# Gated linear attention: output gate multiplied from PSUM by VectorE, norm weights folded into the output projection

## The reference, cut to what matters

```python
o = o_dense + o_sparse
g = (x @ Wga @ Wgb).reshape(B, L, H, DV)
o = o * lax.rsqrt(jnp.mean(o * o, axis=-1, keepdims=True) + EPS) * norm_w
o = o * (g * jax.nn.sigmoid(g))
return o.reshape(B, L, H * DV) @ Wo
```

## Time and profile before

| | |
|---|---|
| median of 3 runs | 1803.05 us (1800.98 to 1803.4) |
| profiled execution, time | 1806.19 us |
| its span, first to last instruction | 1804.9 us |
| TensorE (PE) busy | 1556.2 us, 86% |
| VectorE (DVE) busy | 1275.3 us, 71% |
| ScalarE (ACT) busy | 1098.3 us, 61% |
| GpSimd (POOL) busy | 697.8 us, 39% |
| the GLA stage in the span | about 278 to 941 us |

### The profile page before, as it was taken

The page is one execution under the profiler, slowest core; times in us unless marked ns, Lnnn a source line. Parts: engine busy times, 40 slices in busy tenths (PEclk is TensorE's granted clock), DMA queues, the critical chain, the costliest instruction groups (busy, mean ns, idle before and its releaser), DMA issues. The chain is left out here.

```text
span 1804.9 us, 45554 instructions
## 1 busy us (share of the span) xinstructions
PE 1556.2 (86%) x19648; PEld 998.5 (55%) x19648; DVE 1275.3 (71%) x2003; ACT 1098.3 (61%) x1641; POOL 697.8 (39%) x499
## 2 busy tenths in 40 slices
PE   3587897899999999999977778888788888899999
PEld 2354566787778778877863232433333343466565
DVE  4656644777777677768767868778777886655665
ACT  3255576777767777786752567677667767533331
POOL 4122300554255344534450556365465545411100
PEclk8789898999999999999997889999999999999999
DMA  7864200000000000000024274246237222223332
GB/s 176 196 165 113 47 5 12 2 2 2 2 2 2 2 1 2 2 1 2 32 88 99 52 212 98 63 133 142 56 107 167 66 64 72 67 71 94 95 96 76
DMA packets 54821, 121.17 MB, mean 67 GB/s; under 512 B 6124, under 2 KB 14468, under 8 KB 53020
## 3 DMA queue, kind: packets, MB, share of 16 engines
q1 hardware_dynamic: 51708, 112.74, 23.7%
q10 hardware_dynamic: 2912, 5.51, 1.8%
HBM read 85.70 MB, written 31.74 MB: 65 GB/s over the span
## 5 line engine op out<-in xcount | busy, mean ns | idle before, releaser
L1445 DVE TENSOR_REDUCE arena<-ring 128x2 f32<-128x1024 f32 (+2 forms) x320 | 342.1, 1110 | 87.9 <-PE ring L1302 62.1
L1545 ACT ACTIVATE arena<-ring 128x1024 f32<-128x1024 f32 (+1 forms) x320 | 291.3, 937 | 135.4 <-PE ring L1331 92.0
L1352 PE MATMUL accs<-arena 128*9 128x512 f32 (+3 forms) x1536 | 174.3, 528 | 3.8 <-ACT arena L1545 3.8
L2509 POOL TENSOR_TENSOR arena<-arena 128x1280 f32<-128x1280 f32 x28 | 65.3, 2332 | 287.0 <-PE accs L2270 231.7
L1295 PE MATMUL ring<-arena 48*128 48x512 bf16 (+3 forms) x768 | 128.8, 347 | 41.8 <-DVE arena L1445 21.1
L1324 PE MATMUL ring<-arena 51*128 51x512 bf16 (+3 forms) x768 | 125.0, 343 | 45.8 <-DVE arena L1445 25.1
L2501 POOL TENSOR_TENSOR arena<-arena 128x512 f32<-128x512 f32 x112 | 141.3, 1294 | 3.0 <-DVE arena L2311 3.0
L287 POOL TENSOR_SCALAR xn<-x,moments,rstd 128x128 f32<-128x128 f32 x80 | 65.0, 825 | 192.3 <-DVE rstd L258 178.3
L2782 ACT ACTIVATE arena<-ring 128x512 f32<-128x512 f32 x80 | 47.7, 596 | 134.8 <-PE ring L2651 132.7
L2494 POOL TENSOR_TENSOR arena<-arena 128x1024 f32<-128x1024 f32 x32 | 86.3, 2698 | 108.1 <-DVE arena L2368 108.1
L1718 POOL TENSOR_TENSOR arena<-arena 128x1024 f32<-128x1024 f32 x28 | 65.9, 2354 | 128.6 <-ACT arena L1558 104.5
(11 more groups left out here) (342 smaller groups left out, 4165.9 us busy)
## 6 DMA issues: line engine op xcount, KB each, us to landing
arena<-whole_k SPq DMA_DIRECT2D x32, 512.0 KB, 4.6
arena<-whole_q SPq DMA_DIRECT2D x32, 512.0 KB, 6.2
arena<-moe_scratch SPq DMA_DIRECT2D x128, 128.0 KB, 2.9
arena<-c_scratch_q SPq DMA_DIRECT2D x14, 384.0 KB, 9.3
arena<-c_scratch_k SPq DMA_DIRECT2D x14, 384.0 KB, 12.2
a_scratch_k<-arena SPq DMA_DIRECT2D x8, 512.0 KB, 4.2
c_scratch_k<-arena SPq DMA_DIRECT2D x8, 512.0 KB, 4.5
arena<-a_scratch_q SPq DMA_DIRECT2D x9, 384.0 KB, 7.2
```

The lines of the kernel that those rows point to most:

```text
L1352: mm = nc.tensor.matmul(acc[ci % 2][32 * h:32 * h + HD + 1, a - c * BANK:BANK], c_values[b % 2][:, j, r * HEADS // 2 + 2 * g + i, :], weig ...
L1445: nc.vector.tensor_reduce(dst, src, AX.X, ALU.max, negate=True).then_inc(c_max_taken.up(item), 1)
L1545: nc.scalar.activation(view(c_probs[wi % 4]), view(ps), ACT.Exp).then_inc(c_weights_made.up(item), 1)
```

## The change

After the change ScalarE no longer copies `o`. VectorE multiplies `o`, straight from `accs`, by the gate and writes the product, `opened`, to `o_sb` (L2358 in the changed file). It does so at the item of `in` (or `av` at the first tile of a batch), after ScalarE's square. In `fin` one product of `o_sb` and the inverse root remains (L2407). `norm_w` is multiplied into the rows of the output projection's weights by ScalarE, once, at the stage's start (L2421). TensorE waits for `opened` before it fills `accs`, and for the weights before it projects.

```diff
@@ pe_program, sc (the same line is added in av)
                         if i and t:
                             pe.wait_ge(o_copied, (t - 1, "square"))
+                            pe.wait_ge(o_scaled, (t - 1, "opened"))
@@ pe_program, fin
                         if t:
+                            pe.wait_ge(gate_made, "output weights")
                             pe.wait_ge(o_scaled, (t - 1, "gated"))
@@ dve_program
+                    elif (kind == "in" and item[2] == 1) or (kind == "av" and t % NT == 0):
+                        b, h = half_of(t)
+                        two_rows = lambda ap: ap.rearrange("p (r a c) -> p r a c", r=2, c=P)
+                        if t:
+                            dv.wait_ge(o_scaled, (t - 1, "gated"))
+                        dv.wait_ge(o_copied, (t, "square"))
+                        dv.wait_ge(gate_made, (b, PAIRS - 1))
+                        nc.vector.tensor_tensor(two_rows(o_sb[:, :]), two_rows(accs[:, :])[:, :, 0:2, :],
+                                                gate_T[:, h, :, in_half(t)].rearrange("p (r a) c -> p r a c", r=2),
+                                                ALU.mult).then_inc(o_scaled.up((t, "opened")), 1)
...
                             dv.wait_ge(squared, (t, "inverse"))
-                            nc.vector.scalar_tensor_tensor(r_[:, :], o_sb[:, :], w("b_norm"), r_[:, :], ALU.mult,
-                                                           ALU.mult).then_inc(o_scaled.up((t, "scaled")), 1)
-                            dv.wait_ge(o_scaled, (t, "scaled"))
-                            dv.wait_ge(gate_made, (b, PAIRS - 1))
-                            nc.vector.tensor_tensor(pair_cols(r_[:, :]), pair_cols(r_[:, :]), gate_T[:, h, :, in_half(t)],
-                                                    ALU.mult).then_inc(o_scaled.up((t, "gated")), 1)
+                            dv.wait_ge(o_scaled, (t, "opened"))
+                            nc.vector.tensor_tensor(r_[:, :], o_sb[:, :], r_[:, :], ALU.mult).then_inc(
+                                o_scaled.up((t, "gated")), 1)
@@ act_summed
                 ac.wait_ge(*summed(t))
-                if t:
-                    ac.wait_ge(o_scaled, (t - 1, "scaled"))
-                nc.scalar.activation(both(o_sb[:, :]), src, ACT.Copy).then_inc(o_copied.up((t, "copy")), 1)
@@ act_program
+                ac.wait_ge(weights_in["b"], "all")
+                nc.scalar.activation(w("b_wo"), w("b_wo"), ACT.Copy, scale=w("b_norm")).then_inc(gate_made.up("output weights"), 1)
```

More of the change, by code:

```diff
@@ L2390, in dve_program @@
                         if t < TILES:
-                            b, h = half_of(t)
                             r_ = rs[t % 2]
                             dv.wait_ge(squared, (t, "inverse"))
-                            nc.vector.scalar_tensor_tensor(r_[:, :], o_sb[:, :], w("b_norm"), r_[:, :], ALU.mult,
-                                                           ALU.mult).then_inc(o_scaled.up((t, "scaled")), 1)
-                            dv.wait_ge(o_scaled, (t, "scaled"))
-                            dv.wait_ge(gate_made, (b, PAIRS - 1))
-                            nc.vector.tensor_tensor(pair_cols(r_[:, :]), pair_cols(r_[:, :]), gate_T[:, h, :, in_half(t)],
-                                                    ALU.mult).then_inc(o_scaled.up((t, "gated")), 1)
+                            dv.wait_ge(o_scaled, (t, "opened"))
+                            nc.vector.tensor_tensor(r_[:, :], o_sb[:, :], r_[:, :], ALU.mult).then_inc(
+                                o_scaled.up((t, "gated")), 1)
             def act_summed(t):
```

## The result

| | before | after |
|---|---|---|
| median | 1802.36 us (6 runs) | 1904.3 us (6 runs, 1893.93 to 1908.95) |
| ratio, 95% interval | | 1.057 [1.0547, 1.0593] |
| profiled execution: span | 1804.9 us | 1892.6 us |
| the GLA stage in it | 278.2 to 941.7 = 663.5 us | 264.9 to 1028.1 = 763.2 us |
| ahead of the stage, behind it | 278.2, 863.2 us | 264.9, 864.5 us |

The account below looks back on a forecast made before the run. The gated stage was taken to be paced by TensorE, busy 95% of the time. Terms 85.9 - 15 - 2.1 + 29.6 = +98.4 us on the 1803.05 median gave 1901.5 us, range 1866 to 1924.

Parts of the forecast that it names:

- The chain from `in` to `pair`: VectorE's `opened` ahead of `gk` delays next `pair`: 2.76 us in 26 rounds, 3.53 at four batch heads, +85.9 us.
- The savings at k2 and the gates: One VectorE product less in `fin` shortens TensorE's waits for k2 by 15 us, for the gates by 2.1.
- The copy, the fold, the weights' scaling: Dropping ScalarE's copy of `o`, folding `norm_w` into the weights, scaling them on ScalarE: 0 us each.
- The last tiles: At the stage's end, `state_mid` some 1.3 us later, against 0.5 and 0.75 saved in the final chain: 0.
- The clock: TensorE's granted clock falls after new idle stretches in two rounds of three: 20 x 1.48 = +29.6 us.
- Rival B: TensorE's clock holds in nearly all rounds of the gated stage: sum 68.8, 1872 us; chance 0.22.
- rival C: TensorE's clock falls every round of the gated stage: 1916 us, up to 1928; chance 0.17.
- Rival D: At the round's end the new wait before `pair` is covered, not slower: 1784 us; chance 0.04 including any wash.

Follow-up runs that it names:

- e4: The changed kernel plus matmuls that add no result, filling TensorE's idle time after `in` (10) and at batch heads (18): 1877.74 us, ratio 1.0415.
- e1: The changed kernel with VectorE's `opened` product moved behind `gk`, wait for the square kept: 1794.55 us, ratio 0.9961 to the kernel before.
- e5: The kernel before plus one wait: VectorE waits for ScalarE's copy of the same tile before `factor` and `gk`, no work moved: 1886.63 us, ratio 1.0460.
- e3: The changed kernel with `opened` ahead of ScalarE's square, `gk` still behind `opened`: 1860.81 us, ratio 1.0317 to the kernel before.
- e2: The changed kernel with `gk` ahead of `opened` and `opened` ahead of ScalarE's square: 1787.63 us, ratio 0.9910 to the kernel before.
- e6: The kernel before with only VectorE's product by the gate left out, ScalarE's copy kept: 1787.17 us, ratio 0.9924.
- e7: e2 with the norm's weights multiplied by VectorE in `fin` as before, output projection's weights not scaled: 1784.76 us, ratio 0.9903 to the kernel before.

## Why the prediction was right

1901.5 us was forecast and 1904.3 measured; the sum had +98.4, the medians differ by 102 and the stages by 99.7. To set the steps against the trace I cut the stage at TensorE's starts of `av` (L2258, after the change L2260) and of `pair` (L2189) in each round and compared the pieces with those of before, by hundredths (from tenths, as above, the whole comes to 73.0 and 99.7). Since e4 does all that the change does, but at full clock, it separates the waits from the clock:

| us against before | forecast | e4 | after |
|---|---|---|---|
| `av` to the next `pair`, 30 rounds | +85.9 | +86.8 | +86.8 |
| `pair` to `av` up to tile 30, and the first round's part ahead of it | -17.1, with the clock's 29.6: +12.5 | -15.5 | +11.1 |
| from `av` of tile 30 to the stage's end | 0 | +1.6 | +1.7 |
| whole stage | +98.4 | +72.9 | +99.6 |

- **The chain from `in` to `pair`, +85.9.** Measured 86.8: 2.79 us in the mean of the 26 ordinary rounds (2.76 forecast) and 3.53 in that of the four heads (3.53). e1 shows that its cause is the place in VectorE's queue, e5 that a wait without work is enough, e3 that the loss goes with the length. Whether the wait for the square is needed at all stays open: e2 and e3 exchange the two readers of `accs`, and no run lets them read at once.
- **The savings at k2 and the gates, -15 and -2.1.** Together 15.5 at full clock. By e4's waits 12.1 of it are k2's (17.0 to 4.9) and 2.3 the gates' (5.5 to 3.2). The size was nearly right, the reason only partly named: where nothing hides it (e6), the product less takes 10.5 us off the waits for k2, and the displaced round alone (e5) takes 7.2 off them.
- **The copy, the fold, the weights' scaling, 0 each.** e2 against e6 shows the first, e7 the other two.
- **The last tiles, 0.** Measured +1.7, the one step that was missed. I let a later `state_mid` be paid for by the shorter final chain, but TensorE's wait for GpSimd grew by 1.5, and the low clock came behind it, which the earlier trace rows did not have behind 2.59 us:

```profile
1017.28 1.67 PE L2260 MATMUL accs<-arena 128*64 128x128 f32 x16 [4.13 <-POOL arena L2502]
1018.88 3.45 PE L2272 MATMUL accs<-arena 64*64 64x128 f32 x80
```

  `av` takes 1.67 us for 1.09, `in` 3.45 for 2.41. From the end of `in` to the stage's end, 1.8 came back (7.5 before, 5.7 after). The length of the idling alone does not decide on the clock: at this same place it fell in e1 behind 2.34 us (`in` took 4.08 there) and did not in e2 behind 2.58 (2.41).
- **The clock, +29.6.** It fell behind 21 of the 30 stretches (20 assumed); a fall cost 1.2 us and not 1.48, together 26.7: nearly all of it is the second row's +11.1 less e4's -15.5. The term was right within 3 us, and from 314 to 1028 us the granted clock is 0.95, as forecast. That the count came within one is luck: two rounds of three was a choice between two stretches that disagreed. My 1.48 came from one stretch in which TensorE was busy all through the low clock, and I should have taken it for the upper end. Rival B, the clock holding, would be e4's 1877.7 (1872 by the prediction), and rival C, a fall each time, did not come about. The rule of the Trainium skill ("TensorE: Matmul & The Clock Gate", Part 1), low after idling and released by activity, is borne out by these traces, but the new idle stretches led there only in part, 21 of 30.

Rival D needed `opened` and `gk` to fit before the end of `in`. They can't, but `gk` alone can, and e2 is that version: 1787.6 us, near the 1784 that D gave.

## What to carry to other kernels

On an engine that works its queue in order, an instruction that waits makes everything behind it wait. Before adding one, look at what stands behind it, above all at what empties a PSUM slot, and put that ahead: here the place in the queue was worth 110 us and the work saved 15. Where TensorE sets the pace, count its new idle stretches twice, once for their length and once for the clock behind them (73 and 27 us of the stage here). And when a saving and a wait come in one change, measure the stage for each alone: the saving was real and is kept by exchanging a few lines.

## What the runs showed of the hardware

The clock's dependence on the idle stretch was finer than I had expected: behind stretches of 2.6 to 2.8 us it fell 17 times in 26, of up to 2.1 us (e3) 13 times in 30, and in e2, whose `pair` never waits but for 1.3 us at the heads, it did not fall from 314 us to the stage's end. The same kernel's part ahead of the stage, untouched in all of these, took between 264.9 and 278.2 us in nine profiles; a span can mislead by that much. And GpSimd does not hold VectorE's product from PSUM. The changed kernel can't show it, since GpSimd is idle through all 32 executions of its L2358; but in e2 the same product (L2297) runs beside GpSimd's decay of the state (L2524) in 28 of 32 executions and takes 0.680 to 0.693 us in all 32, where the product of two operands in SBUF took up to 2.86. Its row, and one of the 28:

```profile
L2297 DVE TENSOR_TENSOR arena<-accs,arena x32: 680/692/693, 307.7 to 909.4; 128x512 f32<-128x512 f32 x32
...
581.47 0.69 DVE L2297 TENSOR_TENSOR arena<-accs,arena 128x512 f32<-128x512 f32 x1 [1.27 <-PE accs L2272]
581.51 2.33 POOL L2524 TENSOR_TENSOR arena<-arena 128x1280 f32<-128x1280 f32 x1 [9.11 <-PE accs L2272]
```
